# Sums added to x, layer statistics and gate logits of a mixture of experts: three stages or one, in steps of five tiles

## The reference, cut to what matters

```python
def _layernorm(x, axis=-1, eps=1e-05):
    m = jnp.mean(x, axis=axis, keepdims=True)
    v = jnp.var(x, axis=axis, keepdims=True)
    return (x - m) / jnp.sqrt(v + eps)
...
x = x + _L0_gnn_ref(_layernorm(x, axis=-1), ...)[...]      # + L0_gnn_bias inside
x = x + _L0_ffn_ref(_layernorm(x, axis=-1)[None], ...)[0]  # gate_scores = x @ Wg.T + bg
x = x + _L1_gnn_ref(_layernorm(x, axis=-1), ...)
x = x + _L1_ffn_ref(_layernorm(x, axis=-1)[None], ...)[0]  # logits = x @ gate_w + gate_b
```

## Time and profile before

| what | value |
|---|---|
| median of three runs | 6801.9 us (6800.92 to 6821.01) |
| profiled execution: its own time | 6786.33 us |
| profiled execution: span | 6784.7 us |
| mean granted TensorE clock | 0.805 |
| PE busy | 4343.0 us (64%) |
| DVE busy | 3048.1 us (45%) |
| POOL busy | 2764.5 us (41%) |
| ACT busy | 1972.4 us (29%) |

### The profile page before, as it was taken

The page is one execution under the profiler, slowest core; times in us unless marked ns, Lnnn a source line. Parts: engine busy times, 40 slices in busy tenths (PEclk is TensorE's granted clock), DMA queues, the critical chain, the costliest instruction groups (busy, mean ns, idle before and its releaser), DMA issues. The chain is left out here.

```text
span 6784.7 us, 97259 instructions
## 1 busy us (share of the span) xinstructions
PE 4343.0 (64%) x21805; PEld 3583.0 (53%) x21806; DVE 3048.1 (45%) x6902; ACT 1972.4 (29%) x4303; POOL 2764.5 (41%) x3021
## 2 busy tenths in 40 slices
PE   4666643652996467775776566675676757775392
PEld 3444433542885356664666555564565646664261
DVE  4433457752001645554454544455454445555303
ACT  1111110010231034442444434442444424444120
POOL 2444422533002155553555445553555535553101
PEclk8787766975998588887888788887888878887596
DMA  4555563632453144442444344343443424442131
GB/s 137 158 160 156 159 190 95 176 91 79 184 192 127 35 125 122 116 121 87 116 123 116 88 121 114 108 118 92 116 115 109 117 87 119 121 116 72 47 108 53
DMA packets 461211, 794.76 MB, mean 117 GB/s; under 512 B 221403, under 2 KB 278412, under 8 KB 450551
## 3 DMA queue, kind: packets, MB, share of 16 engines
q0 software_dynamic: 130720, 364.17, 19.4%
q1 hardware_dynamic: 322967, 401.22, 19.0%
q10 hardware_dynamic: 7488, 28.97, 1.4%
HBM read 671.50 MB, written 123.52 MB: 117 GB/s over the span
## 5 line engine op out<-in xcount | busy, mean ns | idle before, releaser
L1730 POOL DMA_INDIRECT g_g<-xl_table,g_idx x2080 | 1968.0, 946 | 1663.3 <-issue 1146.3
L1774 PE MATMUL g_b<-g_onehot,g_msg 128*128 128x128 f32 x8320 | 1375.9, 319 | 893.3 <-DVE agg L1862 336.4
L1774 PEld LDWEIGHTS g_b<-g_onehot,g_msg 128*128 128x128 f32 x8320 | 1296.6, 229 | 1109.8 <-DVE agg L1862 796.8
L1862 DVE TENSOR_TENSOR agg<-agg,g_b 128x256 f32 x2080 | 868.0, 417 | 1331.8 <-remote 854.0
L1761 PE MATMUL g_b<-g_we,g_ea 128*128 128x256 f32 x4160 | 1291.4, 441 | 185.9 <-DVE g_msg L1849 92.4
L1761 PEld LDWEIGHTS g_b<-g_we,g_ea 128*128 128x128 f32 x4160 | 844.8, 225 | 302.0 <-DVE g_msg L1849 112.9
L1833 ACT ACTIVATE g_msg<-g_msg 128x512 f32<-128x512 f32 x1040 | 650.8, 626 | 1124.5 <-DVE g_msg L1849 1002.7
L1849 DVE TENSOR_TENSOR g_msg<-g_g,g_b 128x512 f32<-128x512 f32 x1040 | 710.4, 683 | 483.4 <-remote 222.2
L544 PE MATMUL sc_pe_h<-ae_h_rows,sc_onehot 128*128 x1664 | 506.9, 456 | 218.5 <-DVE sc_prod L616 152.4
L512 POOL DMA_INDIRECT sc_g<-h_table,sc_idx x416 | 399.5, 960 | 452.9 <-DVE sc_alpha L608 330.0
L544 PEld LDWEIGHTS sc_pe_h<-ae_h_rows,sc_onehot 128*128 128x128 f32 x1664 | 348.4, 220 | 332.1 <-issue 272.7
(11 more groups left out here) (256 smaller groups left out, 3536.0 us busy)
## 6 DMA issues: line engine op xcount, KB each, us to landing
g_ea<-in_ea SPq DMA_DIRECT2D x260, 512.0 KB
ex_w<-in_f_w SPq DMA_DIRECT2D x80, 1024.0 KB, 7.4
e_rows<-sc_g SPq DMA_DIRECT2D x208, 272.0 KB
g_g<-xl_table,g_idx POOLq DMA_INDIRECT x2080
at_g<-e_rows ACTq DMA_DIRECT2D x52, 544.0 KB, 4.0
at_g<-e_rows SPq DMA_DIRECT2D x52, 544.0 KB, 3.7
xl_table<-g_rows SPq DMA_DIRECT2D x25, 640.0 KB, 4.0
sc_rel<-rel_row SPq DMA_DIRECT2D x52, 256.0 KB
```

The costliest lines, as they stand in the source:

```text
L1730: nc.gpsimd.indirect_dma_start(out=g.g[:, j, :], out_offset=None, in_=k.xl_table[:, :], in_offset=bass.IndirectOffsetOnAxis(ap=g.idx[:, q, ...
L1774: last = nc.tensor.matmul(ps[u % (SB // 2)][:, at:at + P], g.msg[:, j, b * P:(b + 1) * P], g.onehot[:, j, :], start=True, stop=True)
L1862: nc.vector.tensor_tensor(window, window, ps[u % (SB // 2)][:, i * D:(i + 1) * D] .rearrange("p (b n) -> p b n", b=K), ALU.add).then_inc(g ...
```

## The change

The three stages become one, `gate_inputs`, without hardware loops. Its parts:

- PE transposes `k.agg` or `k.h` straight into three banks `ta`; there is no copy into `part`. In the first call ACT adds the bias in place, in ten operations of 640 columns, before everything else it does.
- DVE adds and takes `bn_stats` tile by tile, then runs the six short operations for each step of five tiles, and a reciprocal and five normalisations for each step. The normalisations of step i stand behind the adds of step i + 1.
- All logits go to columns of one bank `lp`; their bias is added once at the end.
- The gate matrix and the biases are loaded at the start of this one stage, and PE (and ACT, in the first call) waits for them there.

```diff
-def add_features_first(k, tag, src, bias):
...
-def gate_logits(k, ffn):
...
+def gate_inputs(k, ffn, src, src_bias):
+    BANKS = 3
...
+        ta = [bank(f"ta{i}") for i in range(BANKS)]
+        tb = [bank(f"tb{i}") for i in range(BANKS)]
+        lp = bank("lp")
...
+            pe.wait_ge(weights, loads)
+            for t in range(STEP):
+                feature_tile(t)
+            for i in range(NSTEP):
+                if i + 1 < NSTEP:
+                    for j in range(STEP):
+                        feature_tile((i + 1) * STEP + j)
+                for j in range(STEP):
+                    t = i * STEP + j
+                    normal_tile(t)
+                    if t >= 2:
+                        logits_tile(t - 2)
+            for t in range(NT - 2, NT):
+                logits_tile(t)
...
+            if src_bias:
+                act.wait_ge(weights, loads)
+                for i in range(NSTEP):
+                    shift(i)
...
+            add_step(0)
+            for i in range(NSTEP):
+                if i + 1 < NSTEP:
+                    add_step(i + 1)
+                normal_step(i)
+            dve.wait_ge(product, NT)
+            v.tensor_tensor(k.logits[:], lp[:, 0:NT * EX].rearrange("p (t e) -> p t e", e=EX),
+                            bias[:].unsqueeze(1).broadcast_to([P, NT, EX]), ALU.add).then_inc(biased, 1)
...
-def mixture(k, ffn):
-    layer_stats(k, f"ffn{ffn.layer}")
-    gate_logits(k, ffn)
+def mixture(k, ffn, src, src_bias):
+    gate_inputs(k, ffn, src, src_bias)
```

More of the change, by code:

```diff
@@ L1029, in _, with feature_tile, normal_tile, logits_tile @@
         def _(sp):
+            if src_bias:
+                sp.dma_start(col[:], a[src_bias]).then_inc(weights, 16)
             sp.dma_start(w[:], a[ffn.gate_w]).then_inc(weights, 16)
             sp.dma_start(bias[:], a[ffn.gate_b].broadcast_to([P, EX])).then_inc(weights, 16)
+        @block.tensor
+        def _(pe):
+            def feature_tile(t):
+                if src_bias:
+                    pe.wait_ge(shifted, K * (t // STEP) + K)
+                if t >= BANKS:
+                    pe.wait_ge(added, t - BANKS + 1)
+                for b in range(K):
+                    last = nc.tensor.transpose(ta[t % BANKS][:, b * P:(b + 1) * P], src[:, b, t * P:(t + 1) * P],
+                                               k.ident[:])
+                last.then_inc(turned, 1)
+            def normal_tile(t):
+                pe.wait_ge(xn_ready, t + 1)
+                if t >= BANKS:
+                    pe.wait_ge(xt_ready, t - BANKS + 1)
+                for b in range(K):
+                    last = nc.tensor.transpose(tb[t % BANKS][:, b * P:(b + 1) * P],
+                                               xn[:, t // STEP % 2, t % STEP, b * P:(b + 1) * P], k.ident[:])
+                last.then_inc(flipped, 1)
+            def logits_tile(t):
+                pe.wait_ge(xt_ready, t + 1)
+                for b in range(K):
+                    last = nc.tensor.matmul(lp[:, t * EX:(t + 1) * EX], xt[:, t % STEP, b * P:(b + 1) * P], w[:, b, :],
+                                            start=(b == 0), stop=(b == K - 1))
+                last.then_inc(product, 1)
+            pe.wait_ge(weights, loads)
[12 more added lines that the diff above has]
+                logits_tile(t)
@@ new lines, in _, with shift @@
+        @block.scalar
+        def _(act):
+            def shift(i):
+                at = slice(i * STEP * P, (i + 1) * STEP * P)
+                for b in range(K):
+                    nc.scalar.activation(src[:, b, at], src[:, b, at], ACT.Identity, bias=col[:, b:b + 1]
+                                         ).then_inc(shifted, 1)
+            if src_bias:
+                act.wait_ge(weights, loads)
+                for i in range(NSTEP):
+                    shift(i)
+            for i in range(NSTEP):
+                cols = slice(i * STEP, (i + 1) * STEP)
+                act.wait_ge(step, 6 * i + 6)
+                nc.scalar.activation(k.rstd[:, cols], var[:, cols], ACT.Sqrt, bias=k.eps[:, 0:1], scale=1.0 / D
+                                     ).then_inc(rooted, 1)
+                for j in range(STEP):
+                    t = i * STEP + j
+                    act.wait_ge(flipped, t + 1)
+                    if t >= STEP:
+                        act.wait_ge(product, t - STEP + 1)
+                    nc.scalar.copy(xt[:, t % STEP, :], tb[t % BANKS][:, 0:D]).then_inc(xt_ready, 1)
@@ L1047, in _ @@
[L1047 to L1074, removed]
-                for j in range(STEP):
-                    act.wait_ge(turned, it * STEP + j + 1 + STEP)
-                    nc.scalar.copy(xt[:, j, :], tp[j % BANKS][:, 0:D]).then_inc(xt_ready, 1)
+            v = nc.vector
+            def add_step(i):
+                for j in range(STEP):
+                    t = i * STEP + j
+                    dve.wait_ge(turned, t + 1)
+                    v.tensor_tensor(k.x[:, t, :], k.x[:, t, :], ta[t % BANKS][:, 0:D], ALU.add).then_inc(added, 1)
+                    if j > 0:
+                        dve.wait_ge(added, t)
+                        v.bn_stats(st[:, t - 1, :], k.x[:, t - 1, :]).then_inc(stats, 1)
+                t = (i + 1) * STEP - 1
+                dve.wait_ge(added, t + 1)
+                v.bn_stats(st[:, t, :], k.x[:, t, :]).then_inc(stats, 1)
+                n, cols = 6 * i, slice(i * STEP, (i + 1) * STEP)
+                s = st[:, cols, :]
+                dve.wait_ge(stats, (i + 1) * STEP)
+                v.tensor_tensor(k.mean[:, cols], s[:, :, 1], s[:, :, 4], ALU.add).then_inc(step, 1)
+                v.tensor_tensor(diff[:, cols], s[:, :, 1], s[:, :, 4], ALU.subtract).then_inc(step, 1)
+                v.tensor_tensor(var[:, cols], s[:, :, 2], s[:, :, 5], ALU.add).then_inc(step, 1)
+                dve.wait_ge(step, n + 3)
+                v.tensor_scalar(k.mean[:, cols], k.mean[:, cols], 0.5, None, ALU.mult).then_inc(step, 1)
+                v.tensor_tensor(diff[:, cols], diff[:, cols], diff[:, cols], ALU.mult).then_inc(step, 1)
+                dve.wait_ge(step, n + 5)
+                v.scalar_tensor_tensor(out=var[:, cols], in0=diff[:, cols], scalar=D / 4.0, in1=var[:, cols],
+                                       op0=ALU.mult, op1=ALU.add).then_inc(step, 1)
@@ L2102 @@
     graph_layers,
-    lambda k: add_features_first(k, "graph_out", k.h, None),
-    lambda k: mixture(k, FFN[1]),
+    lambda k: mixture(k, FFN[1], k.h, None),
     finish,
```

41 lines of the change are left out of this document (21 added, 20 removed).

## The result

The median is 6741.1 us (6712.8 to 6747.1, four runs) against 6811.5 us before (6800.9 to 6824.6, four runs). The ratio is 0.9888, with a 95% interval of 0.9852 to 0.9923: 1.1% faster, a gain of 52 to 101 us. The forecast was 6704 us with a range to 6738.

What follows compares the result with a forecast made beforehand. Chains of waits, not an engine, bound the two groups of three stages. Merging saves 79 us at the low clock plus 19 from clock rises: 6801.9 - 98 = 6704 us, range 6680 to 6738.

Steps and rivals of the forecast that it cites:

- What bounds the groups, and that their loss comes off the whole: Two groups of three stages (first 107.0 us): chains of waits bind, not an engine; savings come off the whole time.
- Start: Merged stage, loads and ACT's first shifts before PE starts: 5.4 us in the first group, 3.4 in the second.
- First normalised tile: Merged stage, first sums, statistics and normalisation: the first normalised tile reaches PE 10.1 us after PE's start.
- From sums to normalised tile: Between steps, from first transpose of sums to next normalised tile: 5.9 us, three times, 17.7 in all.
- ACT's shifts and the table load: First group, some 9.2 us of ACT work, costed at nothing: covered by under 2 us before the first root.
- A normalised tile: PE as the bound, transposes 0.47 and products 0.86: 1.33 us a tile, 33.2 us for 25 tiles.
- The clock: PE's clock rises inside each gap-free stretch of normalised tiles, saving 9 to 10 us a group, 19 in both.
- The rule of the Trainium skill: Transposes do not count as busy for PE's clock; by it the clock stays low and the time is 6723.
- Low clock throughout, 6723 us: Rival, chance 0.32: eight-column products may not raise PE's clock, so it stays at 0.50 and 79 us are saved.
- High clock: Rival, chance 0.13: PE's clock survives waits between steps and is high nearly throughout; 109 us saved, about 6692.
- no gain: Rival, chance 0.05: without hardware loops, feeding instructions holds PE up and the 79 us are gone.
- The total: Whole kernel: 98 us saved, 79 at low clock and 19 from the clock, giving 6704 us.

Runs made afterwards that it cites:

- e1: The changed kernel again, no edit, on a faster chip: 5486.0 us against 5571.7 for the kernel before, ratio 0.9845.
- e7: Kernel before with only gate_logits changed, all products in one bank and one bias add at the end: ratio 0.9989 to the kernel before.
- e9: Kernel before with two small edits, one logits bank with one bias add and five banks for the sums: ratio 0.9937 to the kernel before.
- e2: Changed kernel with the gate matrix widened to 128 columns (120 of zeros): both groups 146.0 us against 157.8 in e1, one run.
- e4: Changed kernel with PE's transposes of sums mixed between normalised tiles, DVE's and ACT's orders changed too: ratio 0.9799 to the kernel before.
- e5: Changed kernel with the edits of e2 and e4 together: ratio 0.9779 to the kernel before.

## Why the prediction was right and where not

*What bounds the groups, and that their loss comes off the whole:* right for the changed kernel on the faster chip: e1 shows 85.7 us in the whole for 87.6 in the groups. In the first measurement 70 of the 88 arrived, and in e7 and e9 6 of 42 and 36.5 of 85, so it is no rule for every edit.

*Start:* in the first group 5.28 us from the first issue to PE (1470.74 to 1476.02), 5.4 predicted. *First normalised tile:* 9.7 us after it, 10.1 predicted. *From sums to normalised tile:* 5.61, 5.9 predicted. *ACT's shifts and the table load* were covered by 1.8 us, as written: the root ended at 1483.24, DVE's reciprocal came at 1485.06.

*A normalised tile:* 1.33 us predicted, 1.18 measured. I took the span of a lone tile in the earlier trace rows for the pitch of a stream. Back to back, the next tile's first weight load lies under the last product. That is 0.15 us for each of 25 tiles, 3.8 a group. The sum also lacked a wait of 0.68 us ahead of the last step. With the small errors of the terms above, the low clock came to 62.95 and 60.6 us, not 66.9 and 64.9, so that case was worth 87.6, not 79.

*The clock:* the step that failed. "So I expect it to rise inside each stretch, here too" was reasoned from `features_first`, whose PE work is transposes of 128 columns without a gap. The stretches came nearly as described (the last has one gap of 0.68 us), and the clock stayed at 0.50; where it rose in e1, it gained nothing. The 19 us booked for it were not there. e2 shows the predicted pattern of rise and fall once the products are 128 columns wide, with the same order of work: the eight columns, not the shape of the stretch, made the difference. e4 bears it out with over 20 us of PE without a gap at 0.50. It has one rise as well, 2 us behind the first narrow product of its first group, so these products do not keep the clock down in every case. I had named this ground for the low-clock rival and given it a third of the chance.

*The rule of the Trainium skill* ("TensorE: Matmul & The Clock Gate", section on the PE-mode transpose) that transposes do not count as busy for the clock would have had the clock right in the first profile, but by a reason that does not hold. `features_first` rose on transposes alone, and so did the starts of the stage in e2, e4 and e1's second group, before any product, and e9's second `add_features_first`, with a mean of 0.96 over 6297 to 6307 us.

*Low clock throughout, 6723 us:* this is the rival that came true, with 88 us in the groups in place of 79. *High clock, no gain:* neither came; of PE's waits in the two groups none is put down to issue.

*The total:* 98 us predicted, 88 in the groups, 70 between the medians, with an interval of 52 to 101. The difference between 88 and 70 lies outside the groups; it was not in my sum, only in the width of the range, which was 3 us too small at the upper end. Of the 37 us between 6704 and 6741, 10 are that the kernel before took 6811.5 and not 6801.9, 10 are in the groups, and 17 are gain of the groups that did not arrive. The 10 in the groups are the 19 of the clock less the 9 by which the other terms were too dear. That these two errors went against each other was luck: with the groups' true 88 us alone the forecast would have been 6714, inside the range. So the clock is the mechanism that was wrong, but not what carried the time past 6738.

## What to carry to other kernels

Before merging stages, look for the one wait in each that serialises two engines: a bank too few and a bias add in the loop were worth 85 of the 88 us in the groups, though on the slower chip only 36.5 in the whole, for a reason that is open. When one engine works ahead by a step, write down what stands between another engine's two waits: an order of DVE that normalises first was better by 6 to 8 us a stage than one that looks ahead. And judge a local change by its own stretch in the trace, when the rest of the kernel moves by more than the change is worth.

## What the runs showed of the hardware that was not expected

A PE that is busy for 100% of 20 us, with weight loads of 128 columns and products of eight between transposes, stayed at 1.2 GHz (e4, both groups; in the first it had once been at 2.4 GHz for 7 us before). With products of 128 columns in the same order it ran at 2.4 GHz for the last 23 us of each group (e5), and a stage on PE's path became faster by streaming zeros (e2 against e1, 6.5 and 5.3 us).

One program, 22% apart between two chips: 5571.7 and 6817.0 us before the change. The groups of the changed kernel, straight work in SBUF and PSUM, are equal to 0.1 us (after and e1). `attention_edges` takes 568 to 572 us on one and 857 to 877 on the other, the edges of the graph layers 2907 to 2911 and 3819 to 3889. POOL's own part of a gather does not differ (its DMA_INDIRECT rows, mean 946 ns and 949 ns; how long the transfers take these rows do not say). But in a stretch of a graph layer the waits put down to "issue" or to "remote" reach 5 us and more on the slower one. The view of waits there (engine, what waited, its releaser, then total us, times and longest), for the kernel before, whose times are those of the slower chip, and for e1 on the faster one:

```profile
POOL g_g L1730 <- issue: 236.4, 296, 5.5
...
DVE agg L1862 <- remote: 193.3, 41, 7.9
...
ACT g_start L1829 <- remote: 149.6, 24, 18.6
...
DVE agg L1862 <- issue: 46.6, 33, 5.0
```

```profile
POOL g_g L1761 <- issue: 88.4, 290, 0.3
...
DVE agg L1893 <- issue: 28.5, 23, 1.2
```

The first is over 660 us, the second over 480, so the totals are not to be compared, but the longest are. e1's view has no wait on "remote". What these waits are was not tried.
